# A binarized convolution, linear attention and expert layer over 32 images: sixteen chunks of x over four buffers, image 0 loaded ahead of the tables, and the two-term tokens replicated through device memory by five DMAs

## The reference, cut to what matters

```python
x = x + conv(gn(x), gamma, beta, W)     # x: [32, 56, 56, 32] float32
t = x.reshape(32, 3136, 32)             # tokens of 32 channels
t = t + attn(ln(t), wq, wk, wv, dense)  # 16 heads of 32, linear attention
t = t + ffn(ln(t), router, experts)     # 8 experts of 32 x 32, top 2 of softmax
return t.reshape(x.shape)
```

## Time and profile before

| what | value |
|---|---|
| median of 3 runs | 2426.46 us (2424.11 to 2431.5) |
| profiled execution | 2426.23 us, span 2424.4 us |
| PE, PEld busy | 2252.8 us (93%), 1126.0 us (46%) |
| DVE, ACT, POOL busy | 2064.4 (85%), 1589.9 (66%), 1841.0 us (76%) |
| z copies (L470) | 1024 DMAs of 49 KB |
| loads of x for the statistics | 8 DMAs of 1568 KB |

### The profile page before, as it was taken

The page is one execution under the profiler, slowest core; times in us unless marked ns, Lnnn a source line. Parts: engine busy times, 40 slices in busy tenths (PEclk is TensorE's granted clock), DMA queues, the critical chain, the costliest instruction groups (busy, mean ns, idle before and its releaser), DMA issues.

```text
span 2424.4 us, 45391 instructions
## 1 busy us (share of the span) xinstructions
PE 2252.8 (93%) x15908; PEld 1126.0 (46%) x15908; DVE 2064.4 (85%) x2725; ACT 1589.9 (66%) x2789; POOL 1841.0 (76%) x1553
## 2 busy tenths in 40 slices
PE   4369999999999999999999999999999999999971
PEld 4324444444544444444544444454544444454441
DVE  5357899999999999999999999999999999998852
ACT  0157777777777777777777777777777777777620
POOL 0414588888888888888888888888888888888775
PEclk8589999999999999999999999999999999999985
DMA  7421112222221112222221212222211212211001
GB/s 209 112 39 22 32 29 44 35 42 45 45 44 34 36 34 43 34 44 44 45 42 36 34 37 40 35 45 45 45 39 37 37 36 40 36 38 35 21 21 27
DMA packets 284863, 105.31 MB, mean 43 GB/s; under 512 B 246032, under 2 KB 279680, under 8 KB 284512
## 3 DMA queue, kind: packets, MB, share of 16 engines
q1 hardware_dynamic: 284640, 102.41, 21.3%
HBM read 31.19 MB, written 12.85 MB: 18 GB/s over the span
## 4 chain that ended last, share of the span: by engine, by line
PE 67%; DVE 15%; ACT 6%; issue 5%; POOL 3%; DMA 2%; SPq 1%; POOLq 0%; DVEq 0%; ACTq 0%
PE ps L560 15%; PE ps L611 12%; PE ps L551 7%; PE ps L602 6%; PE ps L576 5%; PE ps L585 5%; DVE qbuf L981 4%; DVE prod L1058 4%; ACT ebuf L693 3%; DVE kbuf L975 3%; PE ps L542 2%; PE ps L535 2%; PE ps L630 2%; DVE den L993 2%; PE ps L530 2%
## 5 line engine op out<-in xcount | busy, mean ns | idle before, releaser
L975 DVE SCALAR_TENSOR_TENSOR kbuf<-ps,ebuf 112x1024 f32<-112x1024 f32 x448 | 546.2, 1219 | 114.3 <-ACT ebuf L688 111.8
L693 ACT ACTIVATE ebuf<-ps,small 128x896 f32<-128x896 f32 x448 | 450.3, 1005 | 195.0 <-PE ps L576 113.1
L688 ACT ACTIVATE ebuf<-ps,small 112x1024 f32<-112x1024 f32 x448 | 498.3, 1112 | 107.4 <-PE ps L551 87.8
L981 DVE SCALAR_TENSOR_TENSOR qbuf<-ps,ebuf 128x896 f32<-128x896 f32 x448 | 486.5, 1086 | 43.2 <-ACT ebuf L693 38.7
L802 POOL TENSOR_TENSOR qbuf<-spread_r,qbuf 128x896 f32<-128x896 f32 x224 | 469.0, 2094 | 21.4 <-ACT spread_r L725 21.4
L560 PE MATMUL ps<-kbuf,xcs 112*64 112x512 f32 x1792 | 474.9, 613 | 4.1 <-DVE kbuf L975 4.1
L785 POOL TENSOR_TENSOR rstd<-varr,power 112x28 f32<-112x28 f32 x64 | 307.2, 4800 | 137.7 <-DVE varr L960 137.5
L611 PE MATMUL ps<-qbuf,gmat 128*64 128x224 f32 x3584 | 390.1, 360 | 3.0 <-POOL qbuf L802 2.2
L611 PEld LDWEIGHTS ps<-qbuf,gmat 128*64 128x64 f32 x3584 | 243.7, 138 | 165.0 <-issue 77.8
L1058 DVE TENSOR_TENSOR prod<-ps,gate 112x1024 f32<-112x1024 f32 x224 | 271.2, 1212 | 29.6 <-POOL ffn L847 10.1
L551 PE MATMUL ps<-wk,z 128*112 128x512 f16 x896 | 280.1, 395 | 15.7 <-issue 12.6
(11 more groups left out here) (131 smaller groups left out, 3052.6 us busy)
## 6 DMA issues: line engine op xcount, KB each, us to landing
z<-zhl SPq DMA_DIRECT2D x1024, 49.0 KB, 1.9
qbuf<-in_x SPq DMA_DIRECT2D x8, 1568.0 KB, 8.9
xt<-in_x SPq DMA_DIRECT2D x256, 49.0 KB
out<-ffn SPq DMA_DIRECT2D x256, 49.0 KB
shifted<-nat SPq DMA_DIRECT2D x128, 52.6 KB, 5.0
qbuf<-in_sel SPq DMA_DIRECT2D x1, 1024.0 KB, 13.2
tabn<-in_tabnc SPq DMA_DIRECT2D x1, 784.0 KB, 12.5
p<-in_p2c SPq DMA_DIRECT2D x1, 528.0 KB, 9.6
```

What stands on the lines that cost most here:

```text
L688: act.activation(ebuf[0:PT, 0, :].rearrange("p (a b) -> p a b", a=2), o[0:PT, :, :], ACT.Exp, bias=minus_one[0:PT, :]).then_inc(kexp_made, 1)
L693: act.activation(ebuf[:, 1, 0:2 * G * PT].rearrange("p (a b) -> p a b", a=2), o[:, :, 0:G * PT], ACT.Exp, bias=minus_one).then_inc(qexp_ma ...
L975: v.scalar_tensor_tensor(kbuf[:, n % 2, :].rearrange("p (a b) -> p a b", a=2), o[0:PT, :, :], 1.0, ebuf[0:PT, 0, :].rearrange("p (a b) -> ...
L981: v.scalar_tensor_tensor(qbuf[:, k0:k0 + 2, j, :], o[:, :, 0:G * PT], 1.0, ebuf[:, 1, 0:2 * G * PT].rearrange("p (a b) -> p a b", a=2), AL ...
```

## The change

The statistics take x in sixteen chunks of two images over four buffers; the buffers take the same memory as before. A chunk is issued again into a buffer when the two images in it are turned.

```diff
-        stage = [qflat[0:PT, k * 3584:(k + 1) * 3584].rearrange("p (b f) -> p b f", b=4) for k in range(2)]
+        stage = [qflat[0:PT, k * 1792:(k + 1) * 1792].rearrange("p (b f) -> p b f", b=2) for k in range(4)]
...
-            for q in range(2, 8):
-                sp.wait_ge(stage_turned, 4 * q - 4)
-                sp.dma_start(stage[q % 2], x4[q]).then_inc(stage_in[q % 2], 16)
+            for q in range(4, B // 2):
+                sp.wait_ge(stage_turned, 2 * q - 6)
+                sp.dma_start(stage[q % 4], x2[q]).then_inc(stage_in[q % 4], 16)
```

```diff
+            load(Img(None, 0))
+            for dst, src in ((views["taps"], conv_taps), (views["valid"], validc), (wva_s, wv[0]), (wvb_s, wv[1]), (wd_s, wd)):
+                sp.dma_start(dst, src).then_inc(folds_in, 16)
...
-                if kind == "XT" and n == 0:
+                if kind == "XT" and n == 0 and m.c > 0:
```

```diff
             act.wait_ge(dve_pre, 6)
...
                 elif kind in ("ZT", "ZU"):
                     ln = kind == "ZU"
+                    if m.c == 0 and n == 0 and kind == "ZT":
+                        act.wait_ge(tables_in, 16 * 9)
+                        act.wait_ge(pe_pre, 3)
+                        for v in range(2):
+                            for cs in range(2):
+                                q = slice(64 * v + 32 * cs, 64 * v + 32 * cs + 32)
+                                last = act.activation(p2[q, :, cs, :, 0:C],
+                                                      ps[q, 7, :].rearrange("p (a h o) -> p a h o", a=CH, h=HPC), ACT.Copy,
+                                                      scale=SHIFT)
+                        last.then_inc(act_pre, 1)
```

```diff
+        zd = [nc.dram_tensor(f"zd{k}", [128, 2, PATCHES], F16).ap() for k in (1, 2)]
...
                     sp.wait_ge(zlow_made[ln], m.at(2, 2))
+                    wait(sp, z_in[ln], m.at(64))
+                    sp.dma_start(zd[ln], zhl[ln][:, :, :]).then_inc(z_out[ln], 16)
+                    sp.wait_ge(z_out[ln], m.at(16, 16))
+                    src = zd[ln].rearrange("(g c) h f -> h c g f", g=G)
                     for r in range(4):
-                        for g in range(G):
-                            dst = z2[32 * r:32 * r + 32, g] if ln else z1[32 * r:32 * r + 32, m.par, g]
-                            sp.dma_start(dst.rearrange("p j t -> p (j t)"),
-                                         zhl[ln][32 * g:32 * g + 32, r % 2, :]).then_inc(z_in[ln], 16)
+                        dst = z2[32 * r:32 * r + 32] if ln else z1[32 * r:32 * r + 32, m.par]
+                        sp.dma_start(dst.rearrange("p g j t -> p g (j t)"), src[r % 2]).then_inc(z_in[ln], 16)
```

More of the change, by code:

```diff
@@ L347, in build @@
         eye_in = sem("eye_in")
-        stage_in = [sem(f"stage_in{k}") for k in range(2)]
+        stage_in = [sem(f"stage_in{k}") for k in range(4)]
         stage_turned = sem("stage_turned")
@@ L372, in build @@
         zlow_made = [sem(f"zlow_made{k}") for k in (1, 2)]
+        zd = [nc.dram_tensor(f"zd{k}", [128, 2, PATCHES], F16).ap() for k in (1, 2)]
+        z_out = [sem(f"z_out{k}") for k in (1, 2)]
         z_in = [sem(f"z_in{k}") for k in (1, 2)]
@@ L420, in _ @@
             sp.dma_start(eye_center[:, :], eyec).then_inc(eye_in, 16)
-            x4 = x.rearrange("(q b) h w c -> q b (h w c)", b=4).rearrange("q b (p f) -> q p b f", p=PT)
-            for k in range(2):
-                sp.dma_start(stage[k], x4[k]).then_inc(stage_in[k], 16)
+            x2 = x.rearrange("(q b) h w c -> q b (h w c)", b=2).rearrange("q b (p f) -> q p b f", p=PT)
+            for q in range(4):
+                sp.dma_start(stage[q], x2[q]).then_inc(stage_in[q], 16)
             for dst, src in ((mean4_sb[:, :], mean4), (views["rows"], conv_rows),
@@ L487, in _ @@
             pe.wait_ge(eye_in, 16)
[L488 to L496, removed]
+            for img in range(B):
+                q, b = img // 2, img % 4
+                pe.wait_ge(stage_in[q % 4], 16 * (q // 4) + 16)
+                if img >= 4:
+                    pe.wait_ge(stage_read, img - 3)
+                for j in range(TILES):
+                    dst = ps[:, 2 * b + (j >= 4), (j % 4) * PT:(j % 4 + 1) * PT]
+                    mm = pe.transpose(dst, stage[q % 4][:, img % 2, j * 128:(j + 1) * 128], eye[0:PT, 0:PT])
+                mm.then_inc(stage_turned, 1)
             pe.wait_ge(consts_in, 16 * 5)
@@ L502, in _ @@
             pe.matmul(ps[:, 1, 0:B], mean4_sb[:, :], bw[:, 2, :], start=True, stop=True).then_inc(pe_pre, 1)
-            pe.wait_ge(weights_in, 16 * 11)
+            pe.wait_ge(folds_in, 16 * 5)
             pe.wait_ge(dve_pre, 4)
             for h in range(HEADS):
-                mm = pe.matmul(ps[:, 2, C * h:C * h + C], wvr[:, 128 * h:128 * h + 128], wd_s[:, C * h:C * h + C], start=True, stop=True)
+                mm = pe.matmul(ps[:, 7, C * h:C * h + C], wvr[:, 128 * h:128 * h + 128], wd_s[:, C * h:C * h + C], start=True, stop=True)
             mm.then_inc(pe_pre, 1)
@@ L556, in step @@
                         pe.wait_ge(xcs_made, m.at(2, n // 7 + 1))
+                    if m.c == 0 and n == 0:
+                        pe.wait_ge(act_pre, 1)
                     if n == 0:
@@ L564, in step @@
                 elif kind == "G":
+                    if m.c == 0 and n == 0:
+                        pe.wait_ge(tables_in, 16 * 9)
                     pe.wait_ge(kt_copied, m.at(1, 1))
@@ L647, in _ @@
         def _(act):
[L648 to L655, removed]
-            last.then_inc(act_pre, 1)
             act.wait_ge(dve_pre, 6)
@@ L680, in step @@
                     ln = kind == "ZU"
+                    if m.c == 0 and n == 0 and kind == "ZT":
[8 more added lines that the diff above has]
+                        last.then_inc(act_pre, 1)
                     act.wait_ge(ring_full, no + 1)
-                    wait(act, z_in[ln], m.at(256))
+                    wait(act, z_out[ln], m.at(16))
                     a, b = COL[n]
@@ L984, in step @@
                 elif kind == "DN" and n % 4 == 3:
+                    if m.c == 0 and n == 3:
+                        dve.wait_ge(tables_in, 16 * 9)
                     h = n // 4
```

31 lines of the change are left out of this document (14 added, 17 removed).

## The result

The changed kernel takes 2405.85 us (median of 5 runs, 2402.41 to 2411.39) against 2426.46: ratio 0.991, 95% interval 0.9896 to 0.9925. The forecast was 2404 in a range of 2396 to 2415. The profiled executions are 2405.85 (span 2404.1) and 2426.23 us (span 2424.4), so the traces have 20.3 us to explain.

What follows compares the result with a forecast made beforehand. The prediction took PE's instruction stream to bound the middle, so only PE's waits at opening and z could pay: opening -13.1 and z -9.0 sum to -22.1, from 2426.46 to 2404 us, range 2396 to 2415.

Steps and rivals of the forecast that it cites:

- The budget: Only PE's waits at the opening, the first z and the last z can pay; the middle stays unchanged.
- Part 1: Opening: sixteen chunks of x over four buffers, 2.8 us apart, end the statistics at 60.4 instead of 71.05, -10.65 us.
- rival C: Opening: chunks of x don't stream, 4.33 us each, 12.2 of the gain go, 2416 us; chance 0.06.
- Part 2: Opening: image 0 ahead of the tables, folds apart; PE's wait for ACT goes, -3.75 us, ACT's table load costs +1.3.
- DVE's tail: Opening, DVE's work behind the statistics: some 2 us expected off it, priced at 0 with +1.8 as its end.
- rival A: Opening: folds land 1.9 us after DVE wants them, or DVE's tail doesn't shrink (+1.8); 2406 us; chance 0.11.
- Part 3: z through device memory takes 8.5 us, gaining 3.0 at image 0's ZT and ZU of images 30 and 31; -9.0.
- The estimate 2.9 + 3.8: z's store and reads by the Trainium skill's 2.0 us plus bytes at 436 GB/s; gain 4.7, 2399 in all.
- Rival D: Middle: LG waits for z in every image, 0.9 us in each of 29 images, 27 us; 2445 us; chance 0.05.

Runs made afterwards that it cites:

- opening_only: Changed kernel with the sixteen z copies of before in place of the five DMAs through device memory; 2417.01 us, ratio 0.9953.
- the repetition: Changed kernel run again with no edit, against the kernel before on the same chip; 2404.12 us, ratio 0.9898.
- z_ends_only: Changed kernel with z through device memory for images 0, 29, 30 and 31 alone, sixteen copies for the other 28; 2407.35 us, ratio 0.9921.
- roundtrip_only: Kernel before the change with only the five DMAs of z through device memory added; 2413.76 us, ratio 0.9941.
- chunks_8x4: Changed kernel with x in eight chunks of four images over two buffers again; 2412.01 us, ratio 0.9943.
- the last experiment: Changed kernel with z's store to device memory made three times, one behind the other, for every image; 2472.26 us, ratio 1.0196.
- consts_pause: Changed kernel with the small constants issued ahead of x and a pause of some 29 us ahead of chunk 8; 2427.45 us (one run).

## Why the prediction was right, point by point

**The budget** was right: nothing changed in the middle, and all of the gain lies in the opening, the first z and the end of the run.

**Part 1** was mis-sized: -6.6 us instead of -10.65. The term at fault is the pace of 2.8 us per chunk; the landings from chunk 6 to chunk 15 are (59.76 - 28.58) / 9 = 3.46 apart, 9 x 0.66 = 5.9 us in all. Chunk 6 came 1.8 us earlier than the 30.4 forecast, and that gave part of it back. The pace was read from one pair of landings of before, 49.97 and 55.41, of two chunks that stood queued together behind a pause. In the six kernels with the constants first, early chunks come 2.6 to 2.95 us apart and later ones mostly 3.0 to 3.4, with single gaps of 3.5 to 4.3 where the pace changes and ahead of the last chunk. The size of the term is that of one pair of executions: with the new opening the statistics end at 60.97 in `opening_only` (nearly the 60.4 forecast), 62.88 in the repetition, 64.47 here and 65.62 in `z_ends_only`, with the old one at 71.05 and, in `roundtrip_only`, at 68.69. The pace of chunks 7 to 15 is 3.3 to 3.5 in all four of the new ones, so 2.8 was wrong in each. Nor did DVE's start stay at 20.73, as the prediction had it: the changed kernel's trace shows 18.91, `opening_only` 19.19, the repetition 21.01. Of rival C (4.33 per chunk, 12.2 us) a third came. The rule of the Trainium skill that spoke for rival C, at least 1 MiB per DMA ("DMA: Bandwidth & Descriptors", section "Rules for kernel authors"), did not decide: in `chunks_8x4`, whose loads are above that size, the kernel is slower.

**Part 2** was right to 0.1 us: 3.7 instead of 3.75 for PE's wait for ACT, and 1.2 back for the table load instead of 1.3. DVE's tail shrank as expected (its L933 takes 0.16 us, where L923 took 1.21). The folds were in time: L920 follows L917 at once, at 67.41. That was rival A's first half, and it did not come; nor did it in `opening_only`, where the statistics end at 60.97 and DVE takes up the folds at 63.90 without a wait. So it is not the late statistics that saved it: the last fold there had landed by 61.4 (issued at 57.97, 3.4 us to landing), where the prediction had 62.0. The 3.75 us for image 0 in that figure were a poor reading all the same, since image 0's shifted copies were still in flight in the stretch of the earlier trace rows that gave the 92 GB/s (PE waited for them until 98.92). The shrunken tail hangs on the tables landing behind it, as `chunks_8x4` shows. No run has part 2 alone.

**Part 3**: the path was forecast at 8.5 us and is 8.65, 8.0 and 8.2, but its two terms erred in opposite directions. The store lands in 2.36 us (110.19 to 112.55), not 3.2, and the reads take 6.3 to the first matmul, not 5.15 plus 0.1. The estimate 2.9 + 3.8 from the Trainium skill ("DMA: Bandwidth & Descriptors", section "Anatomy of one DMA") is too long for the store and too short for the reads; the whole is 8.65 where it gives 6.7. The three waits shrank by 2.8, 3.5 and 3.3, 9.6 instead of 9.0.

**What the prediction left out** is the clock. Before, LG of image 29 waited 0.48 us for z, and the matmuls behind it ran slowly; after, it doesn't wait. The same step in the timelines of before and after:

```profile
2267.73 1.58 PE L630 MATMUL ps<-we,z 128*112 128x8 f16 x28 [0.48 <-DMA z<-zhl]
...
2269.64 2.59 PE L611 MATMUL ps<-qbuf,gmat 128*64 128x224 f32 x16
```

```profile
2256.47 1.56 PE L641 MATMUL ps<-we,z 128*112 128x8 f16 x28
...
2258.36 1.73 PE L622 MATMUL ps<-qbuf,gmat 128*64 128x224 f32 x16
```

The wait and its slow stretch account for most of the 0.7 and 1.6 us at image 29, and another 0.8 comes back ahead of image 31's z, most of it in LG of image 30, whose 28 matmuls take 2.04 us instead of 2.74. In the fill 1.3 us are lost, also to slower matmuls: three groups take 1.10, 2.25 and 1.88 us where they took 0.64, 1.71 and 1.08, at a granted clock of 0.67 (168 to 174 and 183 to 187), and others give part of it back. Why the clock stood differently there, behind waits of the same length, no run shows. Of that sum the prediction had nothing; it is +1.8 us net (0.7 + 1.6 + 0.8 - 1.3).

So -22.1 became -20.3: 4.0 less from part 1, 0.6 more from part 3, and 1.8 from the clock and image 29 that no term held; the rest, 0.2, is rounding and the tail. The mechanisms were right, and that the time came within 2 us of 2404 is in part luck: the 4.0 us that part 1 fell short met 2.4 us that part 3 and the clock gave beyond the forecast, and the end of the statistics differs by 4.65 us between the four executions. The lower end of the stated range doesn't follow from its own terms: a z gain of 4.7 takes off 5.1 us and a pace of 2.72 another 0.7, which makes 2398.5 and not 2396. Rival D did not come since the path is 8.2 where 12.3 are available; the last experiment shows that it would have come at 13.5.

## What to carry to other kernels

Price a change to a saturated kernel from the places where its bottleneck engine waits, and then ask at each of them how much spare time lies ahead of the next wait; here 4 us of slack hid a round trip in 28 images that paid in three. Don't take a transfer rate from one pair of landings: read it over a stretch as long as the one that it is used for, and from more than one execution. Small arrays that an engine needs first belong ahead of the large transfers, not behind them; that moved the median by another 2.8 us, with intervals that overlap.

## What the runs showed of the hardware

In the six kernels with the constants first, a full queue of 784 KB loads moved 284 to 303 GB/s for its first seven or eight chunks (275 in `consts_pause`, from 12 to 24 us) and 247 to 262 afterwards, with the DMA engines fully busy in both. Buffers, place in memory, issuing engine, time of start and PE's clock did not change that, and a pause of 29 us brought the rate back for four chunks. The order is not general: in the repetition of the changed kernel the first chunks ran at 264 GB/s and later ones at 287. The cause is not known.

A wait of about 1 us in front of one matmul of a busy PE was followed by matmuls at a reduced granted clock (0.66 over 5 us, between its two levels of 0.50 and 1.00), so that the stall cost more than its length; 0.9 us at 1192.96 in the same run was followed by a stretch at 1.00, so not every stall does it.
